# Cross attention and a routed expert layer on one core: a residual moved to GpSimd, sums ahead of values, and zero products on TensorE

## The reference

```
x = x + xattn(layernorm(x), ctx, ctx)      # softmax(5 * q_norm . k_norm), out of v = ctx
x = x + ffn(layernorm(x))                  # reshaped to 2048 tokens x 512
```

## Time and profile before

| what | value |
|---|---|
| median of 3 runs | 624.82 us (622.26 to 625.44) |
| the profiled execution | 624.58 us, of which the profile's span is 622.8 us |
| PE busy | 568.2 us (91%) |
| DVE, ACT, POOL busy | 354.3 (57%), 281.6 (45%), 187.0 (30%) |
| chain that ended last, by engine | PE 65%, DVE 5%, issue 4%, DMA 1%, POOL 1% |
| DMA traffic | 67.73 MB, mean 109 GB/s |

### The profile page before, as it was taken

How to read it: one execution, slowest core, us unless ns; L and a number is a source line. 1 busy time by engine, 2 the same in 40 slices (tenths; PEclk the granted TensorE clock), 3 DMA queues, 4 the chain that set the end, 5 groups by cost and what they waited for, 6 DMA issues and landing times.

```text
span 622.8 us, 8726 instructions
## 1 busy us (share of the span) xinstructions
PE 568.2 (91%) x2842; PEld 408.5 (66%) x2842; DVE 354.3 (57%) x702; ACT 281.6 (45%) x421; POOL 187.0 (30%) x143
## 2 busy tenths in 40 slices
PE   3999999999998512999999999999999999999994
PEld 2545554554554401788888888888888788888883
DVE  5789998999888684443345443444633354423212
ACT  3777767767777130443333433334334324333220
POOL 8456566566551243100120330300510400500002
PEclk9999999999999655799999999999999999999998
DMA  4523423323213133323332543324451432542001
GB/s 146 196 60 119 137 86 118 126 94 109 96 53 118 52 115 96 95 100 128 97 113 88 183 149 120 118 84 134 152 184 69 137 124 76 190 149 68 0 1 67
DMA packets 46600, 67.73 MB, mean 109 GB/s; under 512 B 8560, under 2 KB 25072, under 8 KB 46576
## 3 DMA queue, kind: packets, MB, share of 16 engines
q1 hardware_dynamic: 42736, 54.84, 26.4%
q0 software_dynamic: 3840, 12.59, 6.2%
HBM read 54.70 MB, written 12.64 MB: 108 GB/s over the span
## 4 chain that ended last, share of the span: by engine, by line
PE 65%; DVE 5%; issue 4%; DMA 1%; POOL 1%; POOLq 0%; DVEq 0%; ACT 0%; SPq 0%
PE two L1423 29%; PE four L1453 9%; PE four L1452 9%; PE four L1450 9%; PE two L1277 2%; PE four L1267 2%; DVE junk L1046 1%; PE two L1289 1%; PE bank_t L1305 1%; DMA x_got<-x2n_dram,idx_all 1%; POOL w_lo L533 1%; DMA p_inv<-inv_dram 0%; PE bank_t L1411 0%; PE bank_m L1411 0%; DVE onehot L1133 0%
## 5 line engine op out<-in xcount | busy, mean ns | idle before, releaser
L759 ACT ACTIVATE h_f<-two 128x512 f32<-128x512 f32 x64 | 38.3, 599 | 231.2 <-PE two L1423 231.2
L1207 DVE TENSOR_TENSOR h_lo<-h_f,h_hi 128x512 fp32r<-128x512 f32 x64 | 44.1, 689 | 125.7 <-ACT h_hi L760 125.7
L1423 PE MATMUL two<-xt_hi,w_hi 128*128 (+1 forms) x256 | 102.9, 402 | 0.7 <-ACT xt_hi L748 0.7
L1423 PE MATMUL two<-xt_hi,w_lo 128*128 (+1 forms) x256 | 101.3, 396 | 0.0
L1453 PE MATMUL four<-w_hi,h_lo 128*128 128x512 f32 x256 | 100.5, 393 | 0.0
L1423 PE MATMUL two<-xt_lo,w_hi 128*128 (+1 forms) x256 | 100.5, 395 | 0.0
L1450 PE MATMUL four<-w_hi,h_hi 128*128 128x512 f32 x256 | 100.5, 392 | 0.0
L1452 PE MATMUL four<-w_lo,h_hi 128*128 128x512 f32 x256 | 100.4, 392 | 0.0
L653 ACT ACTIVATE prob<-four,rnorm 128x512 f32<-128x512 f32 x128 | 77.6, 688 | 28.6 <-POOL rnorm L476 17.6
L1177 DVE TENSOR_TENSOR w_lo<-raw,w_hi 128x2048 fp32r<-128x2048 f32 x30 | 68.7, 2290 | 23.3 <-ACT w_hi L686 23.3
L476 POOL TENSOR_TENSOR rnorm<-ss_max,power 128x8 f32<-128x8 f32 x32 | 64.7, 2024 | 51.5 <-DVE ss_max L808 45.3
(11 more groups left out here) (177 smaller groups left out, 741.5 us busy)
## 6 DMA issues: line engine op xcount, KB each, us to landing
raw<-in_L_ffn_W SPq DMA_DIRECT2D x64, 512.0 KB, 4.0
x_all<-in_x SPq DMA_DIRECT2D x16, 256.0 KB, 2.9
c_sb<-in_ctx SPq DMA_DIRECT2D x16, 256.0 KB, 2.8
out<-x_all SPq DMA_DIRECT2D x16, 256.0 KB, 2.0
x2n_dram<-x2n SPq DMA_DIRECT2D x16, 256.0 KB, 2.0
p_inv<-inv_dram SPq DMA_DIRECT2D x30, 128.0 KB, 2.8
few<-p_sum SPq DMA_DIRECT2D x30, 2.0 KB, 2.2
cst<-in_consts SPq DMA_DIRECT2D x1, 354.5 KB, 5.0
```

The source lines that it names most:

```text
L759: nc.scalar.activation(h_f[m % 2][:, :], z_ps[m % 2][:, :], ACT.Gelu)
L1207: nc.vector.tensor_tensor(h_lo[m % 2][:, :], h_f[m % 2][:, :], h_hi[m % 2][:, :].bitcast(F32), ALU.subtract).then_inc(h_split, 1)
L1423: return nc.tensor.matmul(z[:, :], w_part[c][:, w], x_k, start=start, stop=stop)
```

## The change

On **GpSimd**, a tile of zeros (`idle_in`, 128x512 bf16) is set at the start. The residual of unit 14 moves from DVE to GpSimd (product into `q_f`, addition to x), ahead of `finish` of 14 and of 15, which now follow each other. All four parts of the first chunk's low half are made by GpSimd in rounds 1 to 4 of the search; the second chunk's low half goes to DVE, after expert 0's slots (`split_lo(0, 1)`). In the first unit `key_remainders((0, 1))` waits for the second `widen_queries`.

On **DVE**, `invert_sums` of unit 15 comes first after the last unit, and `residual` of 15 stands ahead of `normalize_x2` of 14. On **ACT**, the copy of unit 15's transposed rows stands ahead of the first count of signs. On **TensorE**, the sums of unit 15 stand ahead of its weighted values of tiles 2 and 3, and batches of products of the zero tile into bank 3 of `four` (128x128 by 128x512, bf16) are put in at 13 places: 10, 7, 5 and 9 in the first unit, 6, 3, 3 and 10 at the end of attention, 9 ahead of `find`, 14 after it, and 2 after each of the first three transposed blocks of tokens. That is 82 products.

```diff
--- before.py
+++ after.py
@@ -164,6 +164,7 @@
         credit = keep("credit", [P, 1])
         x_got = keep("x_got", [P, ST, D])
         o_got = keep("o_got", [P, ST, D])
+        idle_in = keep("idle_in", [P, D], BF16)
         ident = cst[:, C_IDENT:C_IDENT + P]
 
 
@@ -237,6 +238,7 @@
         wg_in = sem("wg_in")
         bg_in = sem("bg_in")
         bf_done = sem("bf_done")
+        idle_set = sem("idle_set")
         x_in = [sem(f"x_in{n}") for n in range(2)]
         c_in = [sem(f"c_in{n}") for n in range(2)]
         power_set = sem("power_set")
@@ -476,6 +478,7 @@
                 return nc.gpsimd.tensor_tensor(dst, src, power[:, 0:n], ALU.pow)
 
             nc.gpsimd.memset(power[:, :], -0.5).then_inc(power_set, 1)
+            nc.gpsimd.memset(idle_in[:, :], 0.0).then_inc(idle_set, 1)
             pool.wait_ge(power_set, 1)
 
             def prepare(u):
@@ -508,6 +511,17 @@
                     pool.wait_ge(sums_ready, number(u))
                 nc.gpsimd.tensor_tensor(half_sum[h][n][:, :], prob[h][2 * n][:, :], prob[h][2 * n + 1][:, :],
                                         ALU.add).then_inc(halves_done[h], 1)
+
+            def residual(u):
+
+                n = number(u)
+                xu = x_all[:, bass.ds(n, 1), :].rearrange("p a d -> p (a d)")
+                pool.wait_ge(o_taken, n + 1)
+                pool.wait_ge(inv_in, 32 * (n + 1))
+                pool.wait_ge(q_split, UNITS)
+                nc.gpsimd.tensor_tensor(q_f[:, :], o_sb[u[1]][:, :], p_inv[u[1]][:, :], ALU.mult).then_inc(on_done, 1)
+                pool.wait_ge(on_done, n + 1)
+                nc.gpsimd.tensor_tensor(xu, xu, q_f[:, :], ALU.add).then_inc(x2_done, 1)
 
             def finish(u):
                 n = number(u)
@@ -523,6 +537,7 @@
             query_norms((0, 0))
             key_norms((0, 0))
             query_norms((0, 1))
+            pool.wait_ge(wq_done, 2)
             key_remainders((0, 1))
             prepare((1, 0))
 
@@ -564,14 +579,12 @@
             run_units(pool, unit)
 
 
+            residual((UNITS // 2 - 1, 0))
             finish((UNITS // 2 - 1, 0))
-            pool.wait_ge(sums_ready, UNITS)
-            for q in range(3):
+            finish((UNITS // 2 - 1, 1))
+            for q in range(4):
+                pool.wait_ge(thr_done, q + 2)
                 first_low(0, q)
-            finish((UNITS // 2 - 1, 1))
-            for q in range(3, 8):
-                pool.wait_ge(thr_done, q - 1)
-                first_low(q // 4, q % 4)
             pool.wait_ge(logit_done, UNITS)
             pool.wait_ge(x2_stored, 16 * UNITS)
             for n in range(2):
@@ -727,6 +740,7 @@
             nc.scalar.activation(key_w[:, 0:EARLY, :, :], key[:, 0:EARLY, :].unsqueeze(3)
                                  .broadcast_to([P, EARLY, E, WAYS]), ACT.Copy).then_inc(key_done, 1)
             take_x2t((UNITS // 2 - 1, 0), bank_m)
+            take_x2t((UNITS // 2 - 1, 1))
 
             def count_signs(r):
 
@@ -736,7 +750,6 @@
 
             act.wait_ge(key_t, 1)
             count_signs(0)
-            take_x2t((UNITS // 2 - 1, 1))
 
             act.wait_ge(margin_done, 2)
             nc.scalar.activation(p_exp[:, :, :], clamped[:, :, :], ACT.Exp, scale=-1.0).then_inc(e_neg, 1)
@@ -862,6 +875,7 @@
                 xu = x_all[:, bass.ds(n, 1), :].rearrange("p a d -> p (a d)")
                 dve.wait_ge(o_taken, n + 1)
                 if late:
+                    dve.wait_ge(x2_done, n)
                     dve.wait_ge(inv_done, late)
                 else:
                     dve.wait_ge(inv_in, 32 * (n + 1))
@@ -1008,12 +1022,11 @@
             put(nc.vector.memset(low[:, :], KEY_LO))
             nc.vector.tensor_scalar(thr[:, :], cst[:, C_KVEC:C_KVEC + 1], width, KEY_LO, ALU.mult, ALU.add
                                     ).then_inc(thr_done, 1)
-            residual(before(end))
+            invert_sums(end)
             statistics_x2(before(end))
-            invert_sums(end)
+            residual(end, 1)
             normalize_x2(before(end), True)
             take_logits(before(before(end)))
-            residual(end, 1)
             statistics_x2(end)
             normalize_x2(end, True)
             take_logits(before(end), bank_m)
@@ -1189,6 +1202,8 @@
                 dve.wait_ge(xthi_done, g + 1)
                 nc.vector.tensor_tensor(lo, bank, hi.bitcast(F32), ALU.subtract).then_inc(xt_split, 1)
 
+            dve.wait_ge(wlo_done, 1)
+            split_lo(0, 1)
             for t in range(ST):
                 dve.wait_ge(xthi_done, t + 1)
                 nc.vector.tensor_tensor(xt_lo[:, 0, :, t * P:(t + 1) * P],
@@ -1306,11 +1321,21 @@
                                             start=(k == 0), stop=(k == KD - 1))
                 last.then_inc(logit_ready, 1)
 
+            def idle_products(n):
+
+                for _ in range(n):
+                    nc.tensor.matmul(four[:, 3, :], idle_in[:, 0:P], idle_in[:, :], start=True, stop=True)
+
+            pe.wait_ge(idle_set, 1)
+            idle_products(10)
             pe.wait_ge(ident_in, 16)
             transpose_queries((0, 0))
             values((0, 0))
+            idle_products(7)
             transpose_queries((0, 1), o_ps[0])
+            idle_products(5)
             spread_queries((0, 0))
+            idle_products(9)
             pe.wait_ge(q_split, 1)
             pe.wait_ge(k_split, 1)
             scores((0, 0), 0, False)
@@ -1350,9 +1375,12 @@
                     scores(after(u), 1, True)
                 if behind > 2:
                     router_logits(before(before(before(u))))
+                if not ahead:
+                    sums(u, behind, ahead)
                 weighted_values(u, 2)
                 weighted_values(u, 3)
-                sums(u, behind, ahead)
+                if ahead:
+                    sums(u, behind, ahead)
 
             run_units(pe, unit)
             end = (UNITS // 2 - 1, 1)
@@ -1371,11 +1399,15 @@
             router_logits(before(before(end)))
             pe.wait_ge(exp_done, TT * UNITS)
             transpose_keys(0, EARLY, 1)
+            idle_products(6)
             transpose_x2(before(end), bank_m)
+            idle_products(3)
             router_logits(before(end), bank_m)
             pe.wait_ge(logit_done, UNITS - 2)
             transpose_x2(end)
+            idle_products(3)
             router_logits(end)
+            idle_products(10)
             transpose_keys(EARLY, UNITS, 2)
             pe.wait_ge(logit_done, UNITS)
             for r in range(ROUNDS):
@@ -1457,9 +1490,12 @@
 
 
             find(0, four[:, 0, :])
+            idle_products(14)
             for t in range(ST):
                 pe.wait_ge(x_gathered[t], 16)
                 transpose_tokens(t, (bank_t, bank_m, *two)[t])
+                if t < ST - 1:
+                    idle_products(2)
             pe.wait_ge(xthi_done, ST)
             pe.wait_ge(xt_split, ST - 1)
             up(0, 0, 0, first=True)
```

## The result

| | median, us | runs | lowest and highest |
|---|---|---|---|
| before | 623.63 | 7 | 622.26 to 625.44 |
| after | 620.37 | 7 | 617.91 to 621.10 |

The ratio of the two is 0.9942, with a 95% interval of 0.9921 to 0.9964: faster, by 0.58%, and by 0.36% at the least. The forecast was 618.2 with a range of 614.5 to 622, so the time is inside the range and 2.2 us above the value. The forecast was counted from the profiled execution of the kernel before, 624.58 us, and the seven runs before have a median of 623.63. So the medians show a gain of 3.26 us of the 6.35 forecast, and a part of the nearness to 618.2 is luck: it comes from the lower base. The profiled execution of the changed kernel took 620.21 us, its span 618.4 against 622.8 before: 4.4 us gained.

A forecast was written before the change was run, and what follows sets the result against it. PE was taken to set the attention loop's pace, DVE close behind, with waiting chains and a slow clock around it. Terms of -2.2, -3.8 and -0.35 (-6.35) from 624.58 gave 618.2 us, range 614.5 to 622.

The forecast's parts named there:

- Part 1: First unit: zero products raise the clock, so scores and the next unit start earlier; -2.2 us, bounds -0.7 and -2.9.
- Part 2: End of attention: earlier reciprocal, residual on POOL and a faster clock bring unit 15's logits and keys forward; -3.8 us.
- Part 3: Ahead of the experts: faster first `up` (-2.1) and last transposes (-0.45), against delayed gathers (+1.0 and +1.2); -0.35 us.
- the load: Ahead of the experts: 1 MB of weights issued beside the gathers delays the fourth one's landing; +1.2 us, bounds 0 and +2.1.
- POOL's hold: Ahead of the experts: DVE's `split_lo(0, 1)` holds POOL's first gather, so all four come late; +1.0 us, bounds 0 and +2.1.
- rival C: Ahead of the experts: DVE's split doesn't hold POOL, as the page's rule says; total 617.2 us, chance 0.10.
- the prediction's own sign of being wrong: At the zero products: the prediction is wrong if PE's batches end later than what PE waits for; no size given.
- The first dozen of `up`: Start of the experts: with the clock up, the first 12 products take 2.8 us, not 5.05; -2.1 us taken.
- A: Ahead of the experts: the clock isn't up for the first `up`, and transposes and `up` stay slow; total 621.1 us, chance 0.18.
- B: Attention loop: DVE sets its pace and takes back what the start won; total 620.4 us, chance 0.15.
- D: First unit: zero products don't raise the clock and stand in the way, scores 4.7 us late; total 625.1 us, chance 0.06.
- E: First unit and end of attention: zero products don't raise the clock at either place; total 632.7 us, chance 0.04.

The follow-up runs named there:

- the experiment with this part alone: The kernel before with only the zero tile, the first unit's 31 products and the wait for `wq_done` added; 622.51 us, ratio 0.9981.
- late split: The changed kernel with DVE's `split_lo(0, 1)` moved from right after the slots to behind the tokens' split; 616.54 us, ratio 0.9869 to the kernel before.

## Why the forecast was right in kind and 2 us short

**Part 1, forecast -2.2.** Mechanism right. Scores at 13.8 forecast and 13.76 found, unit 2 at 20.0 and 20.08, the first sums 2.47 earlier. Two of its steps were off and small. The memset took 0.53 us, above my 0.2 to 0.45, but moved `rstd` only by 0.17. And the wait for `wq_done`, which the step called a help, is worth nothing: `k_lo` holds a DVE cast in its place. In the changed kernel's trace 1.69 survived, in the experiment with this part alone 2.55 to the loop's last unit. But that experiment gained only 1.6 in its span and 0.9 in the median: behind the loop SP's loads for the last unit took 0.7 back, which the forecast didn't price, so -2.2 was too much for the end of the kernel.

**Part 2, forecast -3.8, measured -4.2.** The reciprocal 0.26 after its sums, POOL's operations at 1.27, the normalization of 14 at 0.54, router at 1.05, keys at 0.66: as worked out. The normalization of unit 15 moved by 2.6 (4.27 less the inherited 1.69), as forecast; behind it 1.6 was won and 1.2 forecast. (The sign "within 9 us of the start of the last sums" doesn't follow from the prediction's own moments, which give 206.9 less 196.2, or 10.7; measured were 10.70.) Taken back one at a time, the two moves are worth 0.9 and 1.0: each only goes as far as the other engine's wait. The other moves of this part (`w_lo` away from the normalization of 14, ACT's copy ahead of its count) weren't taken back singly. One thing was missing: the forecast took the clock for granted through the first keys. It held there in the profiled execution, which is luck, and fell in three others of the same code, at 0.9 to 1.7 us each. How often it falls in unprofiled runs isn't known.

**Part 3, forecast -0.35, measured +1.66.** This step failed, and in one term, the load. POOL's hold was priced at +1.0 and measured +1.08, so rival C is refuted. By the Trainium skill (SBUF — State Buffer, section "Who interferes with whom") a DVE `tensor_tensor` leaves a DMA issued by GpSimd alone, which the page marks as inferred; the gather of 2.33 and 2.34 us beside the split, and of 1.24 without it, says otherwise, as the row of before did. The 1 MB load beside the gathers was priced at +1.2, between 0 and +2.1, from the landing of 5.9 against 3.8. It measured 3.06, above the upper bound. The price was put on the fourth gather, and for that one it was right: 1.1, by the landings of the run without pairs. What the forecast put at nothing is that the first gather was hit harder, by 2.7, and that after it PE, and not the fourth landing, was what `up` waited for. While the 512 KB halves filled the DMA engines to 0.92, PE waited 4.45 us; then the clock fell, and the blocks and the pairs ran at the slow pace, 0.9 and 1.08 us. The pairs were put in to hold the clock and counted at nothing; here the prediction's own sign of being wrong came true, that PE's batches end later than what PE waits for.

The last transposes, -0.45 forecast, are there once the split is out of the way: from the gather to `up` the late split needs 9.33 us and the kernel before 9.82, so -0.49. The first dozen of `up` gained 1.99 for the 2.1 taken (it took 2.90, and 4.89 in the trace before, not the 5.05 of the prediction). The terms add up: -0.49 + 1.08 + 3.06 - 1.99 = +1.66.

With +3.06 for +1.2 the forecast would have been 620.1, where the profiled execution took 620.21. That it comes so near is partly luck: in that trace part 1 fell 0.5 short by a stall in the loop, and part 2 won 0.4 more. With the split behind the tokens both costs are gone, and 616.54 was measured.

**The rivals.** A half happened: the clock was down for two of the four token blocks but up for the first `up`. B is refuted for the loop by the start alone. D and E are refuted by the rows at 0.23 each and the transposes at 0.63: products of zeros do raise the clock.

**What stays open.** Why the clock falls at 200 us in some executions and not in others. Why the load of the inverted sums lands between 3.5 and 4.8 us after its issue near 193 to 196 us, which moves POOL's residual and with it the end of attention by about a microsecond. And why the first gather beside the load landed after 6.5 us without products and 7.5 without pairs.

**A better version** is the late split with five more products ahead of the keys: 615.72 us, 1.31% under the kernel before (1.14 to 1.47%) where the change brought 0.58%. The late split alone can't be told from it.

## What to carry to other kernels

A stage that waits for gathers has two covers that look free and aren't: a long VectorE operation beside GpSimd's first gather, and a bulk load that this operation's end releases into the gathers' landing. Ask of each moved instruction what it releases, and when. Price such a load at every transfer that it meets, not at the last one alone: here the first was hit by 2.7 us and the fourth by 1.1, and the engine that waits for the first then has all its own work still ahead of it, perhaps at the slow pace. Work put in to hold the clock pays only while what follows is on time: behind a late transfer, small batches stand in the way at the slow pace.

## What the runs showed of the hardware

- Products of a zero bf16 tile raise the granted clock: ten from 1.36 us on took 3.71 to 4.27 us, nine later ones 2.11, and the first transposes after them took 0.63 and not 1.09.
- Light work can lose the clock or keep it: after a router of 4-column products the granted clock fell from 1.00 to 0.50 at 200 to 202 us in some executions and stayed at 1.00 in others, with the same instructions before it. It cost 0.9 to 1.7 us at the last logits.
- A clock of 1.00 outlasted a wait: PE stood idle for 4.45 us ahead of the first tokens at 1.00, and the clock fell to 0.50 only behind the first block, at 244 us. In the run without pairs it fell within such a wait, at 241 to 242 us.
- A gather issued by GpSimd took 1.24 us by itself and 2.33 beside a VectorE `tensor_tensor` of 2.28 us. Gathers in turn landed after 3.4 to 3.9 us each with neither a load nor a VectorE `tensor_tensor` beside them, and after 7.5, 6.2, 5.5 and 4.9 us with a 1 MB load issued 1.4 us after the first began.
- GpSimd's `k_lo` of 1.3 us stretched the VectorE operation that began beside it: a copy from 0.43 to 1.50, or a cast from 0.22 to 1.31. The statistics of 0.69 us beside the first `k_lo` (6.52 and 6.16 us) weren't stretched.
